# Moving attention's value products one slot back around the score products, and the stabilisers' low part from VectorE to GpSimd

## What is computed

```python
H, DH = (16, 64)
scale = 1.0 / np.sqrt(DH).astype(np.float32)
scores = jnp.einsum('bhqd,bhkd->bhqk', q, k) * scale
attn = jax.nn.softmax(scores, axis=-1)
out = jnp.einsum('bhqk,bhkd->bhqd', attn, v)
out = out.transpose(0, 2, 1, 3).reshape(b, s, H * DH)
out = out @ w_out.T + residual
```

## Time and profile before

| what | value |
|---|---|
| median of three runs | 4191.82 us (4189.85 to 4196.26) |
| the profiled execution, its own time | 4191.36 us |
| its span, first to last instruction | 4189.6 us |
| TensorE busy | 3758.9 us (90%) |
| VectorE busy | 3392.4 us (81%) |
| ScalarE busy | 2623.1 us (63%) |
| GpSimd busy | 3042.9 us (73%) |
| mean granted TensorE clock | 0.952 of full speed |

### The profile page before, as it was taken

How to read it: one execution, slowest core, us unless ns; L and a number is a source line. 1 busy time by engine, 2 the same in 40 slices (tenths; PEclk the granted TensorE clock), 3 DMA queues, 4 the chain that set the end, 5 groups by cost and what they waited for, 6 DMA issues and landing times. The chain is left out here.

```text
span 4189.6 us, 55316 instructions
## 1 busy us (share of the span) xinstructions
PE 3758.9 (90%) x17018; PEld 2903.6 (69%) x17018; DVE 3392.4 (81%) x4389; ACT 2623.1 (63%) x3395; POOL 3042.9 (73%) x2832
## 2 busy tenths in 40 slices
PE   7949977869999999999999999999999999979563
PEld 4635545548888888888888888888888888857321
DVE  6845548869999999999999999999999999946511
ACT  6723333337777777777777777777777777733221
POOL 2456765758888888888888888888888888820155
PEclk9969998979999999999999999999999999989676
DMA  7123437852224332242322423224232242046295
GB/s 271 47 65 60 67 78 244 274 160 63 61 58 89 65 65 60 57 92 62 66 59 59 93 60 67 60 57 91 62 66 59 63 88 61 20 160 221 73 248 111
DMA packets 332634, 396.27 MB, mean 95 GB/s; under 512 B 142541, under 2 KB 251922, under 8 KB 319284
## 3 DMA queue, kind: packets, MB, share of 16 engines
q1 hardware_dynamic: 307702, 362.22, 33.9%
q0 software_dynamic: 24640, 30.52, 4.2%
HBM read 232.47 MB, written 117.79 MB: 84 GB/s over the span
## 5 line engine op out<-in xcount | busy, mean ns | idle before, releaser
L1815 ACT ACTIVATE at_ph<-at_ps_s 128x1024 fp32r<-128x1024 f32 x1024 | 1052.7, 1028 | 637.0 <-PE at_ps_s L1864 621.3
L1724 DVE TENSOR_REDUCE at_mx<-at_ps_u 128x2 f32<-128x1024 f32 x1016 | 1239.8, 1220 | 157.5 <-PE at_ps_u L1847 122.1
L1744 DVE TENSOR_TENSOR at_pl<-at_ps_s,at_ph 128x1024 fp32r<-128x1024 f32 x1024 | 1245.8, 1217 | 18.5 <-ACT at_ps_s L1818 17.4
L1818 ACT ACTIVATE at_ps_s<-at_ps_s 128x1024 f32<-128x1024 f32 x1024 | 1032.2, 1008 | 32.6
L1653 POOL TENSOR_TENSOR at_part<-at_ph,at_vl 128x512 f32<-128x512 f32 x768 | 799.0, 1040 | 114.2 <-ACT at_ph L1815 90.2
L1661 POOL TENSOR_TENSOR at_acc<-at_acc,at_part 128x512 f32<-128x512 f32 x640 | 833.5, 1302 | 50.1
L1879 PE MATMUL at_ps_v<-at_ph,at_va 128*128 128x512 f32 x2048 | 812.2, 397 | 1.1 <-DVE at_pl L1744 1.1
L1880 PE MATMUL at_ps_v<-at_pl,at_va 128*128 128x512 f32 x2048 | 812.9, 397 | 0.0
L1882 PE MATMUL at_ps_v<-at_ph,at_vx 128*128 128x512 f32 x1152 | 456.2, 396 | 0.0
L1880 PEld LDWEIGHTS at_ps_v<-at_pl,at_va 128*128 128x128 f32 x2048 | 387.4, 189 | 90.4
L1863 PE MATMUL at_ps_s<-q,k 128*128 128x512 f32 x1024 | 410.9, 401 | 21.6 <-DVE at_pl L1744 19.5
(11 more groups left out here) (285 smaller groups left out, 5446.3 us busy)
## 6 DMA issues: line engine op xcount, KB each, us to landing
wgu<-Wgu_in SPq DMA_DIRECT2D x64, 384.0 KB, 5.1
qT<-pj_rot SPq DMA_DIRECT2D x32, 512.0 KB, 5.2
vT<-pj_vo SPq DMA_DIRECT2D x16, 1024.0 KB, 5.7
kT<-pj_rot SPq DMA_DIRECT2D x32, 512.0 KB, 3.2
k<-kT SPq DMA_DIRECT2D x32, 512.0 KB, 11.6
q<-qT SPq DMA_DIRECT2D x32, 512.0 KB, 9.5
at_q<-at_low SPq DMA_DIRECT2D x128, 128.0 KB, 2.3
at_vf<-vT SPq DMA_DIRECT2D x32, 512.0 KB, 8.7
```

The source lines that it names most:

```text
L1724: dve.tensor_reduce(mx[:, qb % 2, 2 * i:2 * i + 2], maxima_at(base, j)[:, 0:2], X, ALU.max).then_inc(s["u_max"], 1)
L1744: dve.tensor_tensor(pl[:, n % NP], ps_s[:, n % 2], ph[:, n % NP].bitcast(F32), ALU.subtract)\
L1815: act.activation(ph[:, n % NP], ps_s[:, n % 2], ACT.Exp, scale=DH ** -0.5)\
L1818: act.activation(ps_s[:, n % 2], ps_s[:, n % 2], ACT.Exp, scale=DH ** -0.5)\
```

## The change

GpSimd takes over the subtraction `ml` (`low_stabilisers`): for block 0 ahead of everything else it does in the heads, for the others in slot 2 of the block before, behind that slot's sums. VectorE's `stabilisers` ends with the second reduction. On TensorE the order in slot n becomes V(n-1, first chunk), S(n+2), the fold in a block's second slot, P(n+13), V(n-1, second chunk), with the last slot's values behind the loop. `output` moves from slot 2 to slot 3, `whole` from 5 to 6. One wait is written twice, which does nothing.

```diff
@@ GpSimd
+                def low_stabilisers(block_):
+                    pool.wait_ge(s["mg_ready"], 2 * (block_ + 1))
+                    pool.tensor_tensor(ml[:, block_ % NQB], mg[:], mh[:, block_ % NQB].bitcast(F32), ALU.subtract)\
+                        .then_inc(s["nm_ready"], 1)
+
...
                     for n in range(SLOTS):
                         first_sums(g, hh, n)
-                        if n % PER == 5 and g * NQB + n // PER > 0:
+                        if n % PER == 2 and g * NQB + n // PER + 1 < HEADS * NQB:
+                            low_stabilisers(g * NQB + n // PER + 1)
+                        if n % PER == 6 and g * NQB + n // PER > 0:
                             whole((g * NQB + n // PER - 1) // NQB, (n // PER - 1) % NQB)
...
+                low_stabilisers(0)
                 for i in range(NQB):
                     split_values(0, 0, 0, i)
@@ VectorE, stabilisers
                     dve.tensor_reduce(mh[:, qb], every, X, ALU.max).then_inc(s["mg_ready"], 1)
-                    dve.wait_ge(s["mg_ready"], 2 * (base * NQB + (qb + 1)))
-                    dve.tensor_tensor(ml[:, qb], mg[:], mh[:, qb].bitcast(F32), ALU.subtract).then_inc(s["nm_ready"], 1)
-
@@ ScalarE
-                        if n % PER == 2 and n > PER:
+                        if n % PER == 3 and n > PER:
                             output(pr * 2 + (n - PER) // SLOTS, (n - PER) % SLOTS // PER)
-                        elif n == 2 and pr > 0:
+                        elif n == 3 and pr > 0:
                             output(pr * 2 - 1, NQB - 1)
@@ TensorE
+                def values_at(m, j):
+
+                    values(m // SLOTS, m // SLOTS % 2, m % SLOTS, j)
+
                 def head(pr, hh, prepare):
+
                     g, nxt = pr * 2 + hh, pr * 2 + (hh + 1)
                     for n in range(SLOTS):
+                        m = g * SLOTS + n
+                        if m > 0:
+                            values_at(m - 1, 0)
                         if n + 2 < SLOTS or prepare:
                             scores(g, hh, pr, n + 2, 0)
                             scores(g, hh, pr, n + 2, 1)
-                        values(g, hh, n, 0)
-                        if n % PER == 0 and g * NQB + n // PER > 0:
-                            fold(g * NQB + n // PER - 1)
+                        if n % PER == 1 and m > PER:
+                            fold(m // PER - 1)
                         j = n + PAHEAD
                         if j < SLOTS:
                             products(g, hh, pr, j)
                         elif prepare:
                             products(nxt, 1 - hh, pr + hh, j - SLOTS)
-                        values(g, hh, n, 1)
+                        if m > 0:
+                            values_at(m - 1, 1)
...
+                for j in range(2):
+                    values_at(HEADS * SLOTS - 1, j)
                 fold(HEADS * NQB - 1)
```

More of the change, by code:

```diff
@@ L1904, in head @@
                             products(nxt, 1 - hh, pr + hh, j - SLOTS)
-                        values(g, hh, n, 1)
+                        if m > 0:
+                            values_at(m - 1, 1)
                 for j in range(PAHEAD):
                     products(0, 0, 0, j)
+                pe.wait_ge(s["u_max"], PAHEAD)
                 pe.wait_ge(s["u_max"], PAHEAD)
```

## The result

The changed kernel takes 4351.39 us, the median of four runs (4343.41 to 4357.58), against 4191.28 before: a ratio of 1.038 (95% interval 1.036 to 1.040). It is 160 us slower where 55 us faster was forecast.

What follows compares the result with a forecast made beforehand. TensorE in the attention stage was taken as the bound, losing 2.97 us a head; less 1.25 paid back at cuts, 1.72 times 32 gave 55 us off 4,191.5: 4,137 us, bounds 4,102 to 4,188, range 4,098 to 4,174.

Steps and rivals of the forecast that it cites:

- The floor: TensorE's bare matmul spacing in attention: 84.1 us a head against 87.07 apart, so at most 2.97 to win.
- the stabiliser stalls: TensorE's scores held up by VectorE's subtraction ml and the low part pl after it: two stops of 0.84 us a head.
- (a): Moving ml to GpSimd alone removes the score stalls on pl: 1.7 to 2.3 us a head, 54 to 74 us.
- (b): TensorE's new order: maximum-to-scores path gains 0.47 us of slack; key-query products waiting on maxima keep 0.14, before 0.61.
- (c): VectorE's four cuts a head delay key-query products, most caught behind GpSimd: 1.25 us a head, bounds 0.2 and 1.9.
- (d): GpSimd's added subtraction takes 0.25 us, its stop up to 4.0; cost nothing, bounds 0 to 1 us a head.
- the ring: The exponentials' ring of four buffers: GpSimd's sums must end within 9.5 us, forecast 8.7, so it fits by 0.8.
- It catches up by the head's end: GpSimd, busy 86% of the time, was to make up its lag from the new wait before the head ends.
- the list of signs: What the changed profile would show, including heads 85.4 us apart and GpSimd idle up to 4 us in blocks 0 and 3.
- (e): SP's row DMAs, the later fold and whole, and the kernel's start and end cost nothing; bounds 0 and 3 us in all.
- The slower rival: GpSimd sets the pace in blocks 1 and 2, exponentials waiting on its sums: about 4,297 us, chance 0.06.
- The rival that the contention only moves: Four caught VectorE cuts cost 0.75 us each, 3 us a head, as much as is won: 4,183 to 4,200, chance 0.07.

## Why the prediction was wrong

**The floor and the stabiliser stalls, (a): right.** The scores' wait on pl fell from 91.8 to 6.9 us, and ml moved alone, with the loads behind the rows, took heads from 87.0 to 85.3 us, at the lower end of the 1.7 to 2.3 us forecast.

**The order and its price, (b) and (c): the mechanism right, the size in part luck.** With the row wait taken away, the change has heads of 85.2 us (85.35 forecast) and is 56 us faster than before (55 forecast); the cost that (c) put at the cuts, 1.25 us a head, is 1.1, and goes when the cut moves behind the maximum. But (c) took most of the four cuts as caught, near 1.0 us; one in four was, as in the kernel before, at 1.17, and the others were short. One long and three short cuts cost about what four middling ones were to. In the changed kernel itself the waits on the maxima are less (17.6 us); there no cut is long as a rule (0.42 us in slot 7, 0.58 to 0.67 in the others).

**GpSimd, (d): its own part right, its cover wrong.** The subtraction takes 0.20 us (0.25 forecast), the stop up to 4.0 us (4.0, though the terms given, 2.6 + 1.13 + 1.13 + 1.43 - 2.36, make 3.9), and the ring carries it: exponentials do not wait. Two things failed. "It catches up by the head's end" did not hold: with GpSimd at work 85% of the time (the 86% of the text is 2377.78 of 2790), the stops of slots 2 and 10 still made whole 3.7 us late in slot 30. And "cost nothing, covered by that ring" looked only at who waits for GpSimd's sums. Behind them is also whole, and the only one who waits for whole is SP, whose next orders are the largest transfers of the stage. SP's wait for whole was not looked at. (The stops came in blocks 0 and 1, not in 0 and 3 as the list of signs has it.)

**SP, (e): the step that failed.** It checked when the rows' signal comes and what SP does just ahead of the rows, found both early enough, and put zero to 3 us for the stage. "Fold and whole move by a slot too, each behind what releases it" counted what releases whole and not what whole releases. The real sum: whole a slot later (2.6), GpSimd behind (3.7), scores due earlier (1.7), 8 us in all; 3.5 MB at 211 GB/s are some 17 us, through which a row issued behind them landed only after 10; a slack of 2 us; so 5.7 us of wait and the low clock behind it; heads are 6.9 us over the 85.2, and 6.9 times 31 = 214 us lost on top of a gain of 56, which is the 160 us measured. The sign that the prediction itself had named, TensorE's clock leaving 1.00, came with it.

The slower rival had the right sign and the wrong place: it is not GpSimd that sets the pace. Its mark, exponentials waiting on the sums, is absent. The rival that the contention only moves was not borne out either: it allowed no gain, and with the row wait away the change gains 56 us.

## What to carry to other kernels

When a step is moved that a DMA queue waits for, follow the queue's order past that transfer to the next large one, and ask which small, urgent transfer will fall into its time on the engines; another queue did not help here, starting the burst at another time did. A wait that a profile does not show can have 2 us of slack or 20, and only landing against due time tells. Faster work around a transfer uses up its slack too: 1.7 of the 8 us were the change's own gain. And where two engines' instructions get in each other's way, measure their durations again after every move in the order, as with ml and the cut here: they change with it.

## What the runs showed of the hardware that was not expected

- A 2 KB transfer issued on ScalarE's queue waited as long behind 3.5 MB issued on SP's queue as one on SP's own: 10.2 to 10.8 us to landing against 10.4 to 10.6, where the median is 2.0.
- A stop of TensorE of 5.7 us cost another 1.8 us at the lower clock: nine matmul spacings of 0.43 us. Behind one of 3.5 us (only ml moved, at 1208 us) there were fourteen, of 0.44 us.
- ml on GpSimd is steady (0.19 to 0.20 us in all 128), while the same on VectorE ranged from 0.16 to 1.27 us, and its median moved by a factor of three when another instruction of VectorE changed places.
